# Latent attention: probabilities turned into two f16 parts, three f16 products with the latents, and the loop over head pairs turned by two tiles

## The chip, the cores and the metric

One core of a Trainium2 chip runs the whole kernel in one launch. The metric is the device time of one execution in microseconds (us); the median of several runs is what counts. TensorE multiplies matrices into PSUM, VectorE and ScalarE read PSUM and write SBUF, GpSimd works on SBUF alone, SyncE issues the loads.

## The reference

Two layers, each a gated cross attention followed by a gated feed-forward block, on 4 x 256 tokens of width 256. The change lies in the attention of the second layer, a latent attention with 16 heads over a context of 256 latents of width 64 per batch:

```python
q_big = apply_rope(einsum('bshk,hkq->bshq', (x @ Wq.T), w_kc_q))     # 192 wide per head
kv_r  = apply_rope(kv_c)                                             # latents, 64 wide
q_r   = einsum('bshq,hqr->bhsr', q_big, W_qr)
k_r   = einsum('bld,hdr->bhlr', kv_r, W_kr)
attn  = softmax(einsum('bhsr,bhlr->bhsl', q_r, k_r), axis=-1)
ctx_c = einsum('bhsl,bld->bhsd', attn, kv_r)
ctx   = einsum('bhsd,hkd->bhsk', ctx_c, w_kc_kv)                     # then @ Wo.T
```

## The kernel before

The attention stage treats the heads in 8 pairs `p` (0 to 7) and the 1,024 tokens in 8 tiles `t` of 128 (two tiles for each batch `b`). Every engine has its own program, and within an engine the order is the one written down; a wait for a semaphore holds all that stands behind it on that engine. For one tile of one pair the chain is:

1. TensorE `scores` (L887): four f16 products of 256 columns into bank SC + t % 2.
2. VectorE (L1068): the row minimum `low` of both heads.
3. ScalarE `softmax` (L956): two exponentials with their sums.
4. VectorE (L1073): the reciprocal `inv`.
5. GpSimd `normalise` (L1011): `PB` times `inv`.
6. TensorE `turn` (L896): four transposes of 128 x 128 in f32 into the single bank PTB.
7. ScalarE `turned` (L965): a copy of the bank to `PTS`, f32, which frees the bank (`t_ok`).
8. After two tiles, TensorE `attend` (L904): the latents `KV` (f32, 64 columns) are stationary, `PTS` moves, one product for each half of the tokens and each head; the two heads write the two halves of the partitions of bank CXB.
9. `attended`: ScalarE takes the f16 high part `XCH` (L972), VectorE the rest `XCL` (L1058).

In between, the next pair's queries are made: TensorE `queries` (L863, six f16 products of 512 columns for each tile), VectorE `rotate` (L1030, two multiplications of 96 x 512), GpSimd `rotated` (L1003, two sums), TensorE `to_context` (L876), whose result ScalarE and VectorE split into `Q` (L950, L1049). It runs twice for a pair, for n = 0 (tokens 0 to 511) and n = 1. The weights of the pair after the next are folded in six steps `fold` 0 to 5 (L856) through one PSUM bank, FO. Steps 0, 1 and 5 leave it in two parts: ScalarE takes the high one, VectorE the rest, and VectorE's part releases the next step (`fold_ok`).

The function `pair` gives the order within a pair on each engine. On TensorE, tile t does `scores`, `queries` of the next pair, at t = 1 `to_context` for n = 1, `fold` t (t below 6), at t = 3, 5, 7 `attend` of an earlier batch, and `turn` of tile t - 1. After tile 7 come `to_context` of the next pair for n = 0, `turn` of tile 7 and `attend` of batch 3. On VectorE, tile t does L1068, `rotate`, then L1073, then its shares of `to_context`, `fold` and `attended`. Pair 6 has no folds; pair 7 has neither folds nor queries, and TensorE does products of the output (L130) in their place. In the rows, lines L139 to L160 are the fold products, L182 is VectorE's share of a fold.

## Time and profile before

| | us |
|---|---|
| median of 3 runs | 545.38 (543.02 to 547.01) |
| the profiled execution, time | 546.3 |
| its span, first to last instruction | 544.6 |
| PE busy | 493.6 (91%) |
| DVE busy | 321.5 (59%) |
| ACT busy | 249.2 (46%) |
| POOL busy | 182.0 (33%) |

PE is TensorE, DVE is VectorE, ACT is ScalarE, POOL is GpSimd. The span leaves out 1.7 us around the instructions. The first layer runs up to about 130 us, the attention of the second from there to about 401 us, and its mixture of experts after that. Times in the rows are counted from the start of the span. A matmul's end is modelled and overlaps the next one's start, so that distances between starts tell more than durations.

### The profile page before, as it was taken

To read this page: it belongs to the slowest core of one execution; us is meant where nothing else is said; L and a number is where in the kernel's file an instruction comes from. 1 tells how busy PE (TensorE), PEld (TensorE's weight loads), DVE (VectorE), ACT (ScalarE), POOL (GpSimd) and SP (SyncE) were. 2 spreads that over 40 slices of the span, in tenths; PEclk is the share of its full clock that TensorE was granted. 3 is DMA by queue.
4 is the path that set the end of the run, shared out by engine and by line. 5 is a ranking of instruction groups with operands and counts; after the bars stand their busy time and mean duration, and the time that the engine had idled before them with its cause. 6 is when DMAs were issued, how large, how long until landed. Compare 5 with 4: busy or idle time off the path is not lost. (4 is left out here: it accounts for less than half of the span.)

```text
span 544.6 us, 9443 instructions
## 1 busy us (share of the span) xinstructions
PE 493.6 (91%) x3202; PEld 345.1 (63%) x3202; DVE 321.5 (59%) x881; ACT 249.2 (46%) x598; POOL 182.0 (33%) x181
## 2 busy tenths in 40 slices
PE   4989999986889899998989899898979869999997
PEld 2667878774346555665656566464756536899986
DVE  4998799632567676775767677583456690222202
ACT  4673464452046566665666656565644300322200
POOL 4141220311355566464556646574320000000000
PEclk9996999999799999999999999999999869999999
DMA  8722000000000202020020000000039000088002
GB/s 261 227 66 70 2 1 1 1 2 0 0 1 3 67 1 68 1 67 1 3 64 0 0 0 0 1 1 1 1 110 304 24 1 1 1 255 239 1 1 78
DMA packets 41298, 26.25 MB, mean 48 GB/s; under 512 B 10048, under 2 KB 40816, under 8 KB 41264
## 3 DMA queue, kind: packets, MB, share of 16 engines
q1 hardware_dynamic: 41264, 25.81, 16.3%
q8 instruction: 20, 0.33, 0.2%
q14 instruction: 14, 0.11, 0.1%
HBM read 24.75 MB, written 1.05 MB: 47 GB/s over the span
## 5 line engine op out<-in xcount | busy, mean ns | idle before, releaser
L1014 POOL TENSOR_TENSOR PB<-PB,inv 128x512 f32<-128x512 f32 x64 | 66.5, 1039 | 102.9 <-DVE inv L1073 102.9
L960 ACT ACTIVATE PB<-ps,low 128x256 f32<-128x256 f32 x128 | 59.4, 469 | 54.4 <-DVE low L1068 54.2
L1039 DVE TENSOR_TENSOR TM<-ps,cosq 96x512 f32<-96x512 f32 x64 | 43.8, 684 | 28.1 <-PE ps L870 26.9
L870 PE MATMUL ps<-XH,CH 128*96 128x512 f16 x128 | 49.9, 390 | 2.6 <-POOLq L1001 2.6
L870 PE MATMUL ps<-XL,CH 128*96 128x512 f16 x128 | 49.5, 387 | 0.0
L870 PE MATMUL ps<-XH,CL 128*96 128x512 f16 x128 | 49.5, 387 | 0.0
L1008 POOL TENSOR_TENSOR RO<-TM 96x512 f32<-96x512 f32 x32 | 40.5, 1265 | 21.0 <-DVE TM L1040 21.0
L1068 DVE TENSOR_REDUCE low<-ps 128x2 f32<-128x512 f32 x64 | 43.6, 682 | 3.8 <-PE ps L892 3.4
L909 PE MATMUL ps<-PTS,KV 128*64 128x256 f32 x256 | 34.4, 389 | 11.8 <-ACT PTS L968 11.8
L1040 DVE TENSOR_TENSOR TM<-ps,sinq 96x512 f32<-96x512 f32 x64 | 43.3, 676 | 0.0
L900 PE MATMUL ps<-ident,PB 128*128 128x128 f32 x256 | 40.9, 282 | 0.8 <-ACT PTS L968 0.8
L358 POOL TENSOR_TENSOR HT<-GL,MS 128x512 f32<-128x512 f32 x16 | 20.3, 1278 | 63.8 <-ACT MS L630 48.8
L1054 DVE TENSOR_TENSOR Q<-ps,Q 64x512 f16<-64x512 f32 x32 | 22.0, 689 | 32.6 <-ACT Q L953 32.3
L900 PEld LDWEIGHTS ps<-ident,PB 128*128 128x128 f32 x256 | 28.2, 141 | 20.0 <-issue 14.6
L968 ACT ACTIVATE PTS<-ps 128x512 f32<-128x512 f32 x64 | 38.2, 597 | 5.6 <-PE ps L900 3.9
L1009 POOL TENSOR_TENSOR RO<-TM 96x512 f32<-96x512 f32 x32 | 40.5, 1265 | 0.0
L953 ACT ACTIVATE Q<-ps 64x512 f16<-64x512 f32 x32 | 18.9, 591 | 31.1 <-PE ps L883 30.7
L892 PE MATMUL ps<-KH,Q 128*128 128x256 f16 x128 | 31.5, 273 | 1.6 <-DVE Q L1054 1.6
L539 PE MATMUL ps<-XT,W1T 128*128 128x256 f32 x128 | 32.6, 406 | 0.0
L883 PE MATMUL ps<-RO,M 96*64 96x512 f32 x128 | 31.0, 605 | 1.1 <-POOL RO L1009 1.1
L909 PEld LDWEIGHTS ps<-PTS,KV 128*64 128x64 f32 x256 | 16.2, 136 | 24.5 <-issue 14.5
L892 PE MATMUL ps<-KL,Q 128*128 128x256 f16 x128 | 31.4, 273 | 0.0
(220 smaller groups left out, 994.4 us busy)
## 6 DMA issues: line engine op xcount, KB each, us to landing
EG<-in_L_ffn_W_gate_dram SPq DMA_DIRECT2D x10, 384.0 KB, 4.3
EU<-in_L_ffn_W_up_dram SPq DMA_DIRECT2D x10, 384.0 KB, 5.1
ED<-in_L_ffn_W_down_dram SPq DMA_DIRECT2D x10, 384.0 KB, 5.8
w<-in_L_ffn_W_dram SPq DMA_DIRECT2D x2, 1024.0 KB, 8.3
WQ<-in_L_xattn_Wq_dram SPq DMA_DIRECT2D x8, 256.0 KB, 2.7
WO<-in_L_xattn_Wo_dram SPq DMA_DIRECT2D x8, 256.0 KB, 3.0
WCQ<-in_L_xattn_w_kc_q_dram SPq DMA_DIRECT2D x8, 192.0 KB, 2.7
X<-in_x_dram SPq DMA_DIRECT2D x2, 512.0 KB, 4.0
```

The source lines that it names most:

```text
L870: mm = pe.matmul(g.ps[0:HALF, QA + a, :], cx[:, k, h * DQ + a * HALF:h * DQ + (a + 1) * HALF], xx[:, k, 512 * n:512 * n + 512], start=(k = ...
L892: mm = pe.matmul(g.ps[:, SC + t % 2, S * h:S * h + S], Q[h][u][:, t * P:(t + 1) * P], kx[:, S * (t // 2):S * (t // 2) + S], start=(m == 0) ...
L900: mm = pe.transpose(g.ps[:, PTB, j * P:(j + 1) * P], PB[t % 2][:, j // 2, (j % 2) * P:(j % 2 + 1) * P], g.ident[:, :])
L909: mm = pe.matmul(g.ps[DC * h:DC * h + DC, CXB, 0:S], g.KV[:, 2 * b + j, 0, :], PTS[b % 2][:, 2 * h + j, :], start=(j == 0), stop=(j == 1))
L960: e = act.activation(PB[t % 2][:, h, :], g.ps[:, SC + t % 2, h * S:(h + 1) * S], ACT.Exp, bias=low[:, t % 2, h:h + 1], scale=-1.0, accum_o ...
L968: act.activation(PTS[t // 2 % 2][:, :, (t % 2) * P:(t % 2 + 1) * P], g.ps[:, PTB, :].rearrange("p (j n) -> p j n", j=4), ACT.Copy).then_in ...
L1008: pool.tensor_tensor(RO[:, n, h, 0, :], tm[:, 0, :], tm[:, 2, :], ALU.subtract).then_inc(sum_ok, 1)
L1009: pool.tensor_tensor(RO[:, n, h, 1, :], tm[:, 3, :], tm[:, 1, :], ALU.add).then_inc(sum_ok, 1)
L1014: pool.tensor_tensor(PB[t % 2][:, :, :], PB[t % 2][:, :, :], inv[:, t % 2, :].unsqueeze(2).broadcast_to([P, 2, S]), ALU.mult).then_inc(nor ...
L1039: dve.tensor_tensor(batches(TM[st % 2][:, c, :]), src, over(g.cosq[:, a, :]), ALU.mult)
L1040: dve.tensor_tensor(batches(TM[st % 2][:, s, :]), src, over(g.sinq[:, 1 - a, :]), ALU.mult).then_inc(rope_ok, 1)
L1068: dve.tensor_reduce(low[:, t % 2, :], g.ps[:, SC + t % 2, :].rearrange("p (h s) -> p h s", h=2), AX.X, ALU.min).then_inc(low_ok, 1)
```

## The change

- The turned probabilities leave PSUM as two f16 parts. ScalarE `turned` writes part 0, 256 times the value, in f16; a new VectorE step `turned` writes part 1, the remainder, and only that frees the bank PTB (`t_ok`). ScalarE's copy signals the new semaphore `t_hi`.
- GpSimd makes two f16 parts `KVP` of the latents in the first layer: a copy, and a subtraction ahead of `fold_second`.
- `attend` does three f16 products (high with high, high with low, low with high) where it had one f32 product: 12 instead of 4. `attended` scales back by 1/256 on both engines.
- The loop over pairs is turned by two tiles. A turn of the loop now does tiles 2 to 7 of a pair (`step`) and then tiles 0 and 1 of the next (`cross`). `turn` of tile 7 stands in tile 0 of the next pair, `attend` of batch 3 in tile 1, with the next pair's scores and queries ahead of them.
- `to_context` for n = 0 moves on TensorE and ScalarE from behind tile 7 into tile 5, on VectorE into tile 6.
- Folds 0 to 4 move from tiles 0 to 4 into tiles 3 to 7 on TensorE and ScalarE, fold 5 from tile 5 into tile 0 of the next pair. VectorE's shares of folds 0 and 1 stand in tiles 4 and 5, one tile later than TensorE's.
- On VectorE the order within a tile becomes L1068, the new `turned` of tile t - 2, the reciprocal, and only then `rotate`; then its shares of `to_context`, `fold` and `attended`.

```diff
+UPP = 256.0
...
+                pool.tensor_copy(g.KVP[:, 0, :, :], g.KV[:, :, 0, :]).then_inc(kvp_ok, 1)
...
+                pool.wait_ge(kvp_ok, 1)
+                pool.tensor_tensor(g.KVP[:, 1, :, :], g.KV[:, :, 0, :], g.KVP[:, 0, :, :],
+                                   ALU.subtract).then_inc(kvp_ok, 1)
...
-        PTS = two("PTS", [P, 4, 2 * P])
-        FIRST = 5
+        PTS = two16("PTS", [P, 2, 4, 2 * P])
+        FIRST, AHEAD = 5, 5
...
-        def pairs(eng, body):
-
+        HEAD, TILES = range(0, 2), range(2, NT)
+        LAST = NT - 1
+
+        def pairs(eng, step, cross):
+
+            for t in HEAD:
+                step(0, 0, t, True, False)
             with eng.Fori(0, (PAIRS - 2) // 2, 1) as it:
                 for u in range(2):
-                    body(it * 2 + u, u, True, True)
-            body(PAIRS - 2, 0, False, True)
-            body(PAIRS - 1, 1, False, False)
+                    for t in TILES:
+                        step(it * 2 + u, u, t, True, True)
+                    for t in HEAD:
+                        cross(it * 2 + (u + 1), 1 - u, t, True, True)
+            for t in TILES:
+                step(PAIRS - 2, 0, t, True, False)
+            for t in HEAD:
+                cross(PAIRS - 1, 1, t, False, False)
+            for t in TILES:
+                step(PAIRS - 1, 1, t, False, False)
...
                     for j in range(2):
-                        for h in range(2):
-                            mm = pe.matmul(g.ps[DC * h:DC * h + DC, CXB, 0:S], g.KV[:, 2 * b + j, 0, :],
-                                           PTS[b % 2][:, 2 * h + j, :], start=(j == 0), stop=(j == 1))
+                        for m, (kv, part) in enumerate(((0, 0), (0, 1), (1, 0))):
+                            for h in range(2):
+                                mm = pe.matmul(g.ps[DC * h:DC * h + DC, CXB, 0:S], g.KVP[:, kv, 2 * b + j, :],
+                                               PTS[b % 2][:, part, 2 * h + j, :], start=(j == 0 and m == 0),
+                                               stop=(j == 1 and m == 2))
                     mm.then_inc(cx_ps, 1)
...
-                def pair(p, u, folds, asks):
-                    for t in range(NT):
-                        scores(p, u, t)
-                        if asks:
-                            queries(p + 1, 1 - u, t)
-                        else:
-
-
-                            if t == 0:
-                                pe.wait_ge(cx_ok, 4 * p + CXOK0)
-                            output_share(pe, g, t // 2, range(0, 4) if t % 2 == 0 else range(4, PAIRS - 1))
-                        if t == 1:
-                            to_context(p, u, 1)
-                        if folds and t < 6:
-                            fold(p + 2, u, t)
-                        if t in (3, 5, 7):
-                            attend(p, t // 2 - 1)
-                        if t >= 1:
-                            turn(p, t - 1)
+                def shares(t):
+
+                    output_share(pe, g, t // 2, range(0, 4) if t % 2 == 0 else range(4, PAIRS - 1))
+
+                def step(p, u, t, asks, folds):
+                    scores(p, u, t)
                     if asks:
+                        queries(p + 1, 1 - u, t)
+                    else:
+                        shares(t)
+                    if t == 1:
+                        to_context(p, u, 1)
+                    if t == AHEAD and asks:
                         to_context(p + 1, 1 - u, 0)
-                    turn(p, NT - 1)
-                    attend(p, B - 1)
+                    if folds and t >= 3:
+                        fold(p + 2, u, t - 3)
+                    if t in (3, 5, 7):
+                        attend(p, t // 2 - 1)
+                    if t >= 1:
+                        turn(p, t - 1)
+
+                def cross(p, u, t, asks, folds):
+
+                    scores(p, u, t)
+                    if asks:
+                        queries(p + 1, 1 - u, t)
+                    else:
+                        if t == 0:
+                            pe.wait_ge(rope_ok, 8 * PAIRS + ROPE0)
+                            pe.wait_ge(cx_ok, 4 * p - 2 + CXOK0)
+                        shares(t)
+                    if t == 0:
+                        if folds:
+                            fold(p + 1, 1 - u, FOLDS - 1)
+                        turn(p - 1, LAST)
+                    else:
+                        to_context(p, u, 1)
+                        attend(p - 1, B - 1)
+                        turn(p, 0)
 
                 pe.wait_ge(credit, 1)
                 for t in range(NT):
                     queries(0, 0, t)
                     if t == FIRST:
                         to_context(0, 0, 0)
-                pairs(pe, pair)
+                pairs(pe, step, cross)
+                turn(PAIRS - 1, LAST)
+                attend(PAIRS - 1, B - 1)
...
-                    act.activation(PTS[t // 2 % 2][:, :, (t % 2) * P:(t % 2 + 1) * P],
+                    act.activation(PTS[t // 2 % 2][:, 0, :, (t % 2) * P:(t % 2 + 1) * P],
                                    g.ps[:, PTB, :].rearrange("p (j n) -> p j n", j=4),
-                                   ACT.Copy).then_inc(t_ok, 1)
+                                   ACT.Copy, scale=UPP).then_inc(t_hi, 1)
 
                 def attended(p, b):
                     act.wait_ge(cx_ps, 4 * p + (b + 1 + CXPS0))
                     act.activation(g.XCH[:, bass.ds(p, 1), S * b:S * b + S], g.ps[:, CXB, 0:S],
-                                   ACT.Copy).then_inc(cx_hi, 1)
-
-                def pair(p, u, folds, asks):
-                    for t in range(NT):
-                        softmax(p, t)
-                        if t == 1:
-                            to_context(p, u, 1)
-                        if folds and t < 6:
-                            fold(p + 2, u, t)
-                        if t in (3, 5, 7):
-                            attended(p, t // 2 - 1)
-                        if t >= 1:
-                            turned(p, t - 1)
-                    if asks:
+                                   ACT.Copy, scale=1.0 / UPP).then_inc(cx_hi, 1)
...
+                def step(p, u, t, asks, folds):
+                    softmax(p, t)
+                    if t == 1:
+                        to_context(p, u, 1)
+                    if t == AHEAD and asks:
                         to_context(p + 1, 1 - u, 0)
-                    turned(p, NT - 1)
-                    attended(p, B - 1)
+                    if folds and t >= 3:
+                        fold(p + 2, u, t - 3)
+                    if t in (3, 5, 7):
+                        attended(p, t // 2 - 1)
+                    if t >= 1:
+                        turned(p, t - 1)
+
+                def cross(p, u, t, asks, folds):
+
+                    softmax(p, t)
+                    if t == 0:
+                        if folds:
+                            fold(p + 1, 1 - u, FOLDS - 1)
+                        turned(p - 1, LAST)
+                    else:
+                        to_context(p, u, 1)
+                        attended(p - 1, B - 1)
+                        turned(p, 0)
...
-                    dve.tensor_tensor(g.XCL[:, bass.ds(p, 1), cols], g.ps[:, CXB, 0:S],
-                                      g.XCH[:, bass.ds(p, 1), cols], ALU.subtract).then_inc(cx_ok, 1)
-
-                def pair(p, u, folds, asks):
-                    for t in range(NT):
-                        dve.wait_ge(s_ps, 8 * p + (t + 1))
-                        dve.tensor_reduce(low[:, t % 2, :], g.ps[:, SC + t % 2, :].rearrange("p (h s) -> p h s", h=2),
-                                          AX.X, ALU.min).then_inc(low_ok, 1)
-                        if asks:
-                            rotate(p + 1, t)
-                        dve.wait_ge(exp_ok, 8 * p + (t + 1 + EXP0))
-                        dve.reciprocal(inv[:, t % 2, :], tot[:, t % 2, :]).then_inc(inv_ok, 1)
-                        if t == 1:
-                            to_context(p, u, 1)
-                        if folds and t < 6:
-                            fold(p + 2, u, t)
-                        if t in (3, 5, 7):
-                            attended(p, t // 2 - 1)
+                    dve.scalar_tensor_tensor(out=g.XCL[:, bass.ds(p, 1), cols], in0=g.ps[:, CXB, 0:S],
+                                             scalar=1.0 / UPP, in1=g.XCH[:, bass.ds(p, 1), cols], op0=ALU.mult,
+                                             op1=ALU.subtract).then_inc(cx_ok, 1)
+
+                def lowest(p, t):
+
+                    dve.wait_ge(s_ps, 8 * p + (t + 1))
+                    dve.tensor_reduce(low[:, t % 2, :], g.ps[:, SC + t % 2, :].rearrange("p (h s) -> p h s", h=2),
+                                      AX.X, ALU.min).then_inc(low_ok, 1)
+
+                def inverse(p, t):
+
+                    dve.wait_ge(exp_ok, 8 * p + (t + 1 + EXP0))
+                    dve.reciprocal(inv[:, t % 2, :], tot[:, t % 2, :]).then_inc(inv_ok, 1)
+
+                def turned(p, t):
+
+                    dve.wait_ge(t_hi, 8 * p + (t + 1))
+                    cols = slice((t % 2) * P, (t % 2 + 1) * P)
+                    dve.scalar_tensor_tensor(out=PTS[t // 2 % 2][:, 1, :, cols],
+                                             in0=g.ps[:, PTB, :].rearrange("p (j n) -> p j n", j=4), scalar=UPP,
+                                             in1=PTS[t // 2 % 2][:, 0, :, cols], op0=ALU.mult,
+                                             op1=ALU.subtract).then_inc(t_ok, 1)
+
+                def step(p, u, t, asks, folds):
+                    lowest(p, t)
+                    if t >= 2:
+                        turned(p, t - 2)
+                    inverse(p, t)
                     if asks:
+                        rotate(p + 1, t)
+                    if t == 2:
+                        to_context(p, u, 1)
+                    if t == AHEAD + 1 and asks:
                         to_context(p + 1, 1 - u, 0)
-                    attended(p, B - 1)
+                    if folds and t in (4, 5):
+                        fold(p + 2, u, t - 4)
+                    if t in (4, 6):
+                        attended(p, t // 2 - 2)
+
+                def cross(p, u, t, asks, folds):
+
+                    lowest(p, t)
+                    turned(p - 1, NT - 2 + t)
+                    inverse(p, t)
+                    if asks:
+                        rotate(p + 1, t)
+                    if t == 0:
+                        attended(p - 1, B - 2)
+                        if folds:
+                            fold(p + 1, 1 - u, FOLDS - 1)
+                    else:
+                        attended(p - 1, B - 1)
 
                 dve.wait_ge(credit, 1)
                 dve.wait_ge(g.d_ropeq, 32)
@@ -1087,7 +1170,11 @@
                     rotate(0, t)
                     if t == FIRST + 1:
                         to_context(0, 0, 0)
-                pairs(dve, pair)
+                pairs(dve, step, cross)
+                turned(PAIRS - 1, NT - 2)
+                attended(PAIRS - 1, B - 2)
+                turned(PAIRS - 1, LAST)
+                attended(PAIRS - 1, B - 1)
...
+            g.KVP = mb("KVP", [P, 2, NT, DC], F16)
```

## Rows read from the trace of the kernel before

**Rows 1.** Windows view, attention loop: length, busy us (instructions) per engine, clock, DMA, GB/s

```profile
159.80:393.50 233.70, 220.31 (x1410) 135.69 (x1410) 153.84 (x310) 145.52 (x411) 132.45 (x118) 1.00 0.06 16
```

**Rows 2.** Timeline of TensorE, pair 2: start us, us, instruction, idle before

```profile
223.24 1.94 PE L883 MATMUL ps<-RO,M 96*64 96x512 f32 x8
...
225.11 0.92 PE L139 MATMUL ps<-WCQ,WQ 128*128 128x192 f32 x4
...
226.30 0.27 PE L892 MATMUL ps<-KH,Q 128*128 128x256 f16 x1
...
228.50 0.38 PE L143 MATMUL ps<-ident,WQR 96*128 96x96 f32 x2 [0.30 <-DVE CL L182]
...
229.02 0.66 PE L900 MATMUL ps<-ident,PB 128*128 128x128 f32 x4
...
229.51 0.27 PE L892 MATMUL ps<-KH,Q 128*128 128x256 f16 x1
...
231.77 1.08 PE L909 MATMUL ps<-PTS,KV 128*64 128x256 f32 x8
...
232.79 0.65 PE L900 MATMUL ps<-ident,PB 128*128 128x128 f32 x4
...
240.18 0.27 PE L892 MATMUL ps<-KH,Q 128*128 128x256 f16 x1
...
241.91 0.60 PE L900 MATMUL ps<-ident,PB 128*128 128x128 f32 x4
...
249.71 0.65 PE L909 MATMUL ps<-PTS,KV 128*64 128x256 f32 x4 [1.42 <-ACT PTS L968]
```

**Rows 3.** Timeline of TensorE, pair 3: first score product of tile 2

```profile
258.00 0.27 PE L892 MATMUL ps<-KH,Q 128*128 128x256 f16 x1
```

**Rows 4.** Timeline of VectorE, pair 2, tiles 2, 3 and 6

```profile
228.36 0.68 DVE L1068 TENSOR_REDUCE low<-ps 128x2 f32<-128x512 f32 x1
...
228.96 0.68 DVE L1039 TENSOR_TENSOR TM<-ps,cosq 96x512 f32<-96x512 f32 x1
...
230.15 0.15 DVE L1073 RECIPROCAL inv<-tot 128x2 f32<-128x2 f32 x1
...
230.22 0.67 DVE L1068 TENSOR_REDUCE low<-ps 128x2 f32<-128x512 f32 x1
...
240.82 0.69 DVE L1068 TENSOR_REDUCE low<-ps 128x2 f32<-128x512 f32 x1
```

**Rows 5.** Timeline of VectorE and GpSimd, pair 7, one tile without rotation

```profile
388.94 0.69 DVE L1068 TENSOR_REDUCE low<-ps 128x2 f32<-128x512 f32 x1 [0.24 <-PE ps L892]
...
390.72 0.17 DVE L1073 RECIPROCAL inv<-tot 128x2 f32<-128x2 f32 x1 [1.09 <-ACT PB L960]
...
390.96 1.04 POOL L1014 TENSOR_TENSOR PB<-PB,inv 128x512 f32<-128x512 f32 x1 [1.14 <-DVE inv L1073]
```

**Rows 6.** Groups by line, VectorE, attention loop: busy us, mean ns, idle before

```profile
L1054 DVE TENSOR_TENSOR Q<-ps,Q 64x512 f16<-64x512 f32 x30 | 20.7, 689 | 32.6 <-ACT Q L953 32.3
...
L182 DVE SCALAR_TENSOR_TENSOR CL<-ps,CH 128x384 f16<-128x384 f32 x11 | 6.1, 551 | 0.4
...
L182 DVE SCALAR_TENSOR_TENSOR NL<-ps,NH 128x256 f32 x6 | 2.4, 400 | 0.0
```

**Rows 7.** Timeline: pair 0's tile 2 on TensorE, and the last VectorE row of the stage

```profile
162.88 0.27 PE L892 MATMUL ps<-KH,Q 128*128 128x256 f16 x1
...
400.33 0.42 DVE L1062 TENSOR_TENSOR wide<-ps,wide 128x256 f16<-128x256 f32 x1 [3.33 <-ACT wide L974]
```

**Rows 8.** Timeline of GpSimd in the first layer

```profile
24.84 4.31 POOL L349 TENSOR_SCALAR wide<-X,mix 128x256 f32<-128x256 f32 x8 [11.82 <-DVE mix L732]
...
31.64 0.92 POOL L368 TENSOR_TENSOR CL<-FS,CH 128x384 f16<-128x384 f32 x1 [2.49 <-ACT FS L614]
```

**Rows 9.** Windows view around a fall of TensorE's clock, columns as in rows 1

```profile
36.70:40.10 3.40, 1.18 (x9) 0.73 (x7) 3.36 (x15) 2.39 (x7) 1.57 (x3) 1.00 0.70 193
...
40.00:56.00 16.00, 15.08 (x70) 11.72 (x71) 13.39 (x56) 6.38 (x12) 2.52 (x3) 0.68 0.25 74
```

More of the change, by code:

```diff
@@ L1016, in normalise @@
                                        ALU.mult).then_inc(norm_ok, 1)
-                def pair(p, u, folds, asks):
-                    for t in range(NT):
-                        normalise(p, t)
-                        if asks and t % 2 == 1:
-                            rotated(p + 1, t // 2)
+                def step(p, u, t, asks, folds):
+                    normalise(p, t)
+                    if asks and t % 2 == 1:
+                        rotated(p + 1, t // 2)
+                def cross(p, u, t, asks, folds):
+                    step(p, u, t, asks, folds)
                 for st in range(4):
                     rotated(0, st)
-                pairs(pool, pair)
+                pairs(pool, step, cross)
             @block.vector
@@ L1084, in _, with cross @@
+                def cross(p, u, t, asks, folds):
+                    lowest(p, t)
[9 more added lines that the diff above has]
+                        attended(p - 1, B - 1)
                 dve.wait_ge(credit, 1)
```

15 lines of the change are left out of this document (8 added, 7 removed).

## The prediction

> **What bounds the kernel now.** I read the windows view of the attention loop first. TensorE is busy 220.3 of 233.7 us at full clock, VectorE 153.8 (66%) [rows 1]. Then the timeline of one pair on TensorE: the reader is to see that its blocks follow each other almost without a gap and that the pattern repeats after 258.00 - 226.30 = 31.70 us [rows 2, 3]. Distances between starts give the price of each block. A plain tile (240.18 to 241.91) has scores and queries, S+Q = 1.73, for 4 x 256 + 6 x 512 = 4,096 columns, which makes 0.108 for 256 columns in f16. The others are to_context 1.87 (223.24 to 225.11), fold 1 0.75 (225.11 to 226.30 less one turn of 0.44), fold 2 0.52, turn 0.49 (229.02 to 229.51), attend 1.02 (231.77 to 232.79) [rows 2]. The one large gap is 1.42 us at 249.71, at the end of the pair, where attend of batch 3 waits for ScalarE's copy; there is one of 0.30 at fold 2 [rows 2]. Each gap is about 0.16 longer than shown, because of the modelled end of the matmul before it, so about 2.0 us of a pair are idle. So TensorE bounds the loop, at 29.7 us of work in 31.7.
>
> VectorE is the engine to look at next. Where work is queued, its big steps start 0.60 apart: minimum 0.60, the two multiplications of rotate 1.19, reciprocal 0.07, a tile in 1.86 [rows 4]. The time that matters is the one hidden there: in pair 7, where no rotate stands between them, the reciprocal starts 1.78 after the minimum, of which 1.09 is a wait for ScalarE's exponentials [rows 5]. Before, rotate fills that wait.
>
> **The change part by part.**
>
> TensorE's work. An attend of now runs its two heads side by side: each f32 instruction takes twice 0.108 for 256 columns, eight would need 1.73 in a row, and the block takes 1.02 = 4 x 0.215 + 0.16 [rows 2]. Twelve f16 products side by side make 6 x 0.108 + 0.17 = 0.83; one behind the other they would make 12 x 0.108 + 0.17 = 1.47. No row shows f16 products of 64 columns. I take 0.83, by the attend row, since only the type differs, and keep 1.47 as a bound. This takes 4 x 0.19 = 0.8 us of work from a pair. The turned order also puts scores and queries between turn 7 and attend 3, so that the gap at the end of a pair loses its cause. If TensorE still bounded the loop, a pair would take 29.7 - 0.8 = 28.9.
>
> VectorE's work. The new turned has 512 columns. The same instruction takes 0.400 with 256 and 0.551 with 384 [rows 6], so 0.70, or 0.61 from start to start. ScalarE's copy and its 64 instructions stay as they are.
>
> VectorE's order. What costs is where the reciprocal stands. A tile is now minimum (0.60), turned (0.61), then the rest of the wait for the exponentials: the reciprocal starts 1.80 after the minimum whatever turned costs between nothing and 1.2, then rotate. That is 1.80 + 0.07 + 1.20 = 3.07 a tile against 1.86 [rows 4, 5]. Turned is hidden; rotate no longer is. The extras follow behind rotate: to_context 1.38 [rows 6], fold 0.48, fold 5 and attended 0.37 each. Without any wait for TensorE a pair costs VectorE 8 x 3.07 + 2 x 1.38 + 2 x 0.48 + 0.37 + 4 x 0.37 = 30.1 us, more than TensorE's 28.9 and near the 31.7 of now.
>
> The fold chain. TensorE's fold 1 stands in tile 4 and needs `fold_ok` of fold 0, which VectorE gives behind rotate of tile 4, because its share stands one tile later. With L for the start of VectorE's minimum (0.64 after the start of scores, 240.18 to 240.82 [rows 2, 4]), TensorE has its queries out at L + 1.09 and then holds until L + 3.07 + 0.56 + 0.06 = L + 3.69. Queued behind are fold 1, turn 3 and the scores of tile 5, for which VectorE waits in turn. So the two engines take turns instead of overlapping: the next minimum comes at 3.69 + 0.75 + 0.49 + 0.64 = 5.57. Tile 5 repeats it with fold 2, with to_context hidden in the wait: 3.69 + 0.52 + 0.83 + 0.49 + 0.64 = 6.17. Without these two holds the tiles would take 3.44 and 3.96.
>
> A pair, minimum to minimum, is then: tile 2 4.45 (3.07 and to_context); tile 3 3.31 (attend needs turned of tile 1, at L + 1.35, then 0.83 + 0.49 + 0.64); tile 4 5.57; tile 5 6.17; tile 6 4.80 (3.07, to_context, attended); tile 7 3.31; next tile 0 3.81 (3.07, attended, fold 5); next tile 1 3.99 (VectorE waits for attend 3 behind to_context, then ScalarE's part). The sum is 35.4 us, 3.7 more than now.
>
> The stage. It runs from the minimum of tile 2 in pair 0 (162.88 + 0.64 = 163.5) to 400.75, 237.2 us [rows 7]. Pair 0's first tiles lose their two folds, which brings that start to 162.9. Then six turns of the loop, 6 x 35.4 = 212.5; the rest of pair 6 without folds, 4.45 + 3.31 + 3.44 + 3.96 + 4.80 + 3.31 = 23.3; pair 7, without rotate, at 2.48 a plain tile (1.35 for turned, 0.49, 0.64) and 3.31 one with attend: 2.48 + 4.59 + 3 x 2.48 + 2 x 3.31 = 21.1 up to its last minimum, and then 7.8 for the last chain (minimum, exponentials, norm, turn, ScalarE's copy, turned, attend, both attended). The end is 162.9 + 212.5 + 23.3 + 21.1 + 7.8 = 427.6, 26.8 us later than now.
>
> What costs nothing. The two new GpSimd steps of the first layer lie before waits of 11.8 and 2.5 us, and the dearer one should be near 1.2 (0.92 with 384 columns) [rows 8]; uncovered they would cost 2. Loads of the fourth and later pairs start after fold 5, which comes some 11 us later, and still have nine tiles before fold 0 wants them; that cover is over 25 us. Everything behind the stage is as it was.
>
> **A rule of the skill against the change.** The 1.02 of the attend row leaves no room for loads of the stationary latents between products [rows 2]. The Trainium skill (TensorE: Matmul & The Clock Gate, Part 3) says that a load overlaps running products only where the row groups differ, and here both heads use all rows. By it each of twelve loads of 64 columns at its P/1.2 ns, 53 ns, would stand in the open, and attend would come to an estimated 1.47, by chance the bound above. The f32 row does not bear that out, so I leave it to the second rival.
>
> **The rivals.**
>
> 1. TensorE stays the bound and the turned loop gives back the gaps: 28.9 a pair, six pairs 17 us, some 3 more in the last two: 526. It needs rotate or the reciprocal not to hold up the minimum of the next tile. For it speaks that TensorE is 94% busy; against it that the order on VectorE is fixed and its chain alone takes 30.1. Chance 0.05.
> 2. Attend runs head after head, 1.47 instead of 0.83. It lies on the path in tiles 3, 5, 7 and 1: 4 x 0.64 x 7 = 18 us, 590. Chance 0.10.
> 3. TensorE's clock falls in the new holds of 2.5 us. In 36.7 to 40.1 TensorE was busy 1.18 of 3.40 us, mostly with transposes, and the clock stood at its lower level, 1.2 GHz, for about 10 us after it (0.68 over 16 us) [rows 9]. The 1.42 us gap at 249.71 had no such effect; the clock of the loop is 1.00 [rows 1, 2]. The new hold is longer than both, but has dense products on both sides. Each fall would cost 2 to 5 us; three in six pairs make 6 to 15, so 578 to 587. Chance 0.20.
> 4. The fold chain holds nobody, because VectorE's share comes before TensorE asks for it. Then tiles 4 and 5 cost 3.44 and 3.96, a pair 31.1, and the gain in the loop pays for the last chain: 26 us less than my sum, 546. Against it: fold 0 on VectorE stands behind the very scores that TensorE issues just before fold 1. Chance 0.07.
>
> **How the numbers follow.** The profiled execution was 546.3, so my sum is 546.3 + 26.8 = 573.1. The median stands 0.9 lower, and I forecast 572. Errors of 0.1 us in each tile's chain would make 5 us. Chance of this case, 566 to 579, 0.58. Range 562 to 591: it takes in rivals 2 and 3 and leaves out 1 and 4. Slower by over 1% (about what a measurement of this kernel can tell from no change): 0.58 + 0.10 + 0.20 = 0.88. Within 1%: most of rival 4, 0.06. Faster by over 1%: rival 1 and the rest of 4, 0.06.
>
> **What the changed profile would show.** Pairs repeat after about 35.4 us. TensorE's busy share of the loop falls from 94% to about 82%, with two holds in each pair before fold 1 and fold 2, released by VectorE's L182 step, the first near 2.5 us. VectorE has a wait of about 0.5 for ScalarE before each reciprocal and a rotate behind it. The attend block takes 0.83. The end of a pair has no gap. I am wrong if the reciprocal comes much sooner than 1.8 after the minimum, if the fold holds are short, or if scores of the next tile wait for something other than VectorE. The last chain of pair 7 should be about 2 us longer than now.

## The result and the profile after

The changed kernel takes 590.0 us (median of 4 runs, 589.0 to 594.4), and the kernel before took 546.2 beside it (4 runs, 543.0 to 551.4): a ratio of 1.083, 95% interval 1.076 to 1.090. The ratio leaves out the run of 551.4, in which the kernel before was in a slower state. The profiled execution took 594.4 with a span of 592.7; its mean granted clock was 0.941, that of the other runs 0.949 to 0.952, which fits its 4 us above the median.

The page of the changed kernel, its first two parts cut to the lines used here, and then the row of the clock from the page of the kernel before:

```profile
span 592.7 us, 9779 instructions
...
PE 503.8 (85%) x3330; PEld 357.3 (60%) x3330; DVE 365.8 (62%) x945; ACT 246.8 (42%) x596; POOL 184.4 (31%) x183
...
PEclk9997999996988988988999899998898997999999
```

```profile
PEclk9996999999799999999999999999999869999999
```

TensorE is busy for 10 us more but in a span that is 48 longer. Each digit of the clock's row is a fortieth of the span, 14.8 us in the changed kernel, whose loop lies in the 12th to the 27th. The kernel before has nines throughout its loop (clock 1.00 in [rows 1]); the changed one has seven eights there. The windows view of the six turns of the loop, from the minimum of tile 2 in pair 0 to that of pair 6, and of the stretches before and after one fall of the clock (columns as in rows 1):

```profile
163.80:393.90 230.10, 189.42 (x1221) 118.74 (x1219) 162.43 (x308) 116.57 (x331) 110.10 (x98) 0.93 0.06 16
...
211.00:214.40 3.40, 0.89 (x5) 0.33 (x3) 2.89 (x7) 1.02 (x4) 2.77 (x3) 1.00 0.00 0
215.40:218.80 3.40, 3.40 (x13) 1.59 (x11) 1.46 (x3) 1.91 (x6) 0.42 (x1) 0.55 0.00 0
```

TensorE is busy 82% of the loop (94% before), and with a granted clock of 0.93 one clock in fourteen is missing. VectorE in the same pattern, tiles 4 and 5 of pair 5 (timeline; compare [rows 4, 5]). L1120 is the minimum, L1132 the new turned, L1126 the reciprocal, L1090 and L1091 rotate, L183 the fold share; the cut row is the share of attended, L1113:

```profile
364.51 0.69 DVE L1120 TENSOR_REDUCE low<-ps 128x2 f32<-128x512 f32 x1 [0.31 <-PE ps L910]
365.12 0.68 DVE L1132 SCALAR_TENSOR_TENSOR PTS<-ps,PTS 128x512 f16<-128x512 f32 x1
366.29 0.17 DVE L1126 RECIPROCAL inv<-tot 128x2 f32<-128x2 f32 x1 [0.49 <-ACT PB L998]
366.48 0.69 DVE L1090 TENSOR_TENSOR TM<-ps,cosq 96x512 f32<-96x512 f32 x1
367.08 0.68 DVE L1091 TENSOR_TENSOR TM<-ps,sinq 96x512 f32<-96x512 f32 x1
367.68 0.54 DVE L183 SCALAR_TENSOR_TENSOR CL<-ps,CH 128x384 f16<-128x384 f32 x1
...
370.70 0.69 DVE L1120 TENSOR_REDUCE low<-ps 128x2 f32<-128x512 f32 x1 [2.15 <-PE ps L910]
```

The reciprocal starts 1.78 after the minimum and waits 0.49, rotate follows it, and after its shares of fold and attended VectorE stands for 2.15 us. TensorE over the same time (L910 scores, L888 queries, L140 fold 1, L918 turn, L928 attend; compare [rows 2]):

```profile
362.61 0.84 PE L928 MATMUL ps<-PTS,KVP 128*64 128x256 f16 x12 [1.81 <-DVE PTS L1132]
363.38 0.66 PE L918 MATMUL ps<-ident,PB 128*128 128x128 f32 x4
...
365.39 0.38 PE L888 MATMUL ps<-XH,CL 128*96 128x512 f16 x1
368.28 0.92 PE L140 MATMUL ps<-WCQ,WQ 128*128 128x192 f32 x4 [2.51 <-DVE CL L183]
369.03 0.78 PE L918 MATMUL ps<-ident,PB 128*128 128x128 f32 x4
369.61 0.42 PE L910 MATMUL ps<-KH,Q 128*128 128x256 f16 x1
369.82 0.42 PE L910 MATMUL ps<-KL,Q 128*128 128x256 f16 x1
```

Fold 1 is held for 2.51 us and starts 0.06 after VectorE's share ends: the two engines take turns. From 369.6 on the scores start 0.21 apart where 0.11 is usual: the clock is at its lower level. The attend block takes 0.77, from 362.61 to the start of the turn at 363.38. The longest waits of the loop (waits view, 163.8 to 393.9: who waited for whom, us in total, times, longest):

```profile
DVE low L1120 <- PE ps L910: 33.1, 24, 3.1
...
PE ps L928 <- DVE PTS L1132: 21.6, 12, 1.8
...
PE ps L140 <- DVE CL L183: 14.5, 6, 2.5
```

### The profile page after: what moved, and what is told of

The parts are those of the page before. It is cut to its first block and busy times, and to the rows that moved or that the text cites. A ratio compares the mean times of both kernels' runs of the same rounds, so it can differ in the third digit from the quotient of the medians.

```text
span 592.7 us, 9779 instructions
## 1 busy us (share of the span) xinstructions
PE 503.8 (85%) x3330; PEld 357.3 (60%) x3330; DVE 365.8 (62%) x945; ACT 246.8 (42%) x596; POOL 184.4 (31%) x183
## 5 line engine op out<-in xcount | busy, mean ns | idle before, releaser
L1063 POOL TENSOR_TENSOR PB<-PB,inv 128x512 f32<-128x512 f32 x64 | 66.5, 1039 | 140.4 <-DVE inv L1126 140.4
L1120 DVE TENSOR_REDUCE low<-ps 128x2 f32<-128x512 f32 x64 | 44.0, 687 | 41.2 <-PE ps L910 40.8
L888 PE MATMUL ps<-XH,CH 128*96 128x512 f16 x128 | 53.7, 420 | 2.7 <-POOLq L1050 2.6
L928 PE MATMUL ps<-PTS,KVP 128*64 128x256 f16 x384 | 28.7, 288 | 29.9 <-DVE PTS L1132 29.9
L888 PE MATMUL ps<-XL,CH 128*96 128x512 f16 x128 | 53.2, 415 | 0.0
L1090 DVE TENSOR_TENSOR TM<-ps,cosq 96x512 f32<-96x512 f32 x64 | 43.9, 686 | 14.4 <-PE ps L888 12.8
L888 PE MATMUL ps<-XH,CL 128*96 128x512 f16 x128 | 52.4, 409 | 0.0
L918 PE MATMUL ps<-ident,PB 128*128 128x128 f32 x256 | 43.6, 295 | 7.3 <-DVE PTS L1132 7.2
L1132 DVE SCALAR_TENSOR_TENSOR PTS<-ps,PTS 128x512 f16<-128x512 f32 x64 | 43.7, 682 | 2.9 <-ACT PTS L1006 2.6
L928 PEld LDWEIGHTS ps<-PTS,KVP 128*64 128x64 f16 x384 | 20.2, 114 | 39.9 <-issue 28.7
L1091 DVE TENSOR_TENSOR TM<-ps,sinq 96x512 f32<-96x512 f32 x64 | 43.3, 677 | 0.0
L1006 ACT ACTIVATE PTS<-ps 128x512 f16<-128x512 f32 x64 | 38.1, 596 | 11.9 <-PE ps L918 10.7
L918 PEld LDWEIGHTS ps<-ident,PB 128*128 128x128 f32 x256 | 29.1, 146 | 22.4 <-issue 22.2
L910 PE MATMUL ps<-KH,Q 128*128 128x256 f16 x128 | 34.9, 296 | 1.5 <-DVE Q L1105 1.5
L910 PE MATMUL ps<-KL,Q 128*128 128x256 f16 x128 | 35.1, 296 | 0.0
```

Of the source, the lines that this page charges most:

```text
L888: mm = pe.matmul(g.ps[0:HALF, QA + a, :], cx[:, k, h * DQ + a * HALF:h * DQ + (a + 1) * HALF], xx[:, k, 512 * n:512 * n + 512], start=(k = ...
L910: mm = pe.matmul(g.ps[:, SC + t % 2, S * h:S * h + S], Q[h][u][:, t * P:(t + 1) * P], kx[:, S * (t // 2):S * (t // 2) + S], start=(m == 0) ...
L918: mm = pe.transpose(g.ps[:, PTB, j * P:(j + 1) * P], PB[t % 2][:, j // 2, (j % 2) * P:(j % 2 + 1) * P], g.ident[:, :])
L928: mm = pe.matmul(g.ps[DC * h:DC * h + DC, CXB, 0:S], g.KVP[:, kv, 2 * b + j, :], PTS[b % 2][:, part, 2 * h + j, :], start=(j == 0 and m == 0),
L1063: pool.tensor_tensor(PB[t % 2][:, :, :], PB[t % 2][:, :, :], inv[:, t % 2, :].unsqueeze(2).broadcast_to([P, 2, S]), ALU.mult).then_inc(nor ...
L1090: dve.tensor_tensor(batches(TM[st % 2][:, c, :]), src, over(g.cosq[:, a, :]), ALU.mult)
```

## Experiments

The tiles below are distances between starts of VectorE's minimum, in us, taken from the timeline. Each row is one pair of the loop as it ran, and the row of e1 is the one pair of its loop without a fall of the clock.

```
tile                       2     3     4     5     6     7    next 0  1     pair
forecast                  4.45  3.31  5.57  6.17  4.80  3.31  3.81  3.99   35.4
changed kernel, pair 4    4.73  3.45  6.23  6.57  5.05  3.31  3.85  4.36   37.6
e10 (holds filled), 2     4.73  3.45  5.59  6.09  5.04  3.32  3.85  4.35   36.4
e1 (shares early), 3      4.70  3.52  3.96  4.27  5.05  3.31  3.98  4.41   33.2
e4 (rotate first), 2      4.01  3.45  5.08  5.58  4.54  3.32  3.31  4.89   34.2
e5 (both), 2              4.00  3.45  3.45  4.86  4.53  3.32  3.31  4.89   31.8
e6 (both, f32 parts), 5   3.94  2.63  2.96  4.91  4.54  2.28  3.32  4.89   29.5
```

The row of the changed kernel has one fall of the clock in it, in tile 4. Times of pairs differ by some tenths with the clock and between even and odd pairs.

**e1: VectorE's fold shares one tile earlier.**

```diff
-                    if folds and t in (4, 5):
-                        fold(p + 2, u, t - 4)
+                    if folds and t in (3, 4):
+                        fold(p + 2, u, t - 3)
```

> VectorE takes its share of folds 0 and 1 one tile earlier, in the tile in which TensorE makes them. Theory (TensorE and VectorE take turns at folds 1 and 2): the two holds vanish, tiles 4 and 5 take about 3.6 and 4.1 us from minimum to minimum where they took 6.2 and 6.7, six pairs give some 31 us back with the clock falls that followed the holds: about 558. Rival (the new VectorE step turned, or the late rotate, is what costs): 580 or more. Rival (the clock falls come anyway and are the main loss): 575 to 590, with as many falls as before.

569.5 us, ratio to the kernel before 1.044 (1.040 to 1.048), so 20.5 less than the changed kernel, where 31 were expected. The holds went, and tiles 4 and 5 took 3.96 and 4.27, near the 3.6 and 4.1 expected. What stayed are falls of the clock, now at the wait of attend in tile 7: five from pair 0 to pair 5 and one in pair 6, where the changed kernel had nine and two. A pair with one took 34.5 to 34.9 where the table shows 33.2 for the one without. The theory of the hold stands. The rival about the falls is right in that they come without the hold, but about half of them went, and the time lies below its 575.

**e2 and e10: the holds filled.** Before fold 1 TensorE does ten products of 512 columns into the idle bank QP; e10 also does five before the attend of tile 7. Nobody reads them.

```diff
+                    if folds and t == 4:
+                        for k in range(10):
+                            pe.matmul(g.ps[:, QP, :], g.XH[:, 0, 0:P], g.XH[:, 1, 0:512], start=True, stop=True)
                     if folds and t >= 3:
                         fold(p + 2, u, t - 3)
+                    if folds and t == 7:                                  # e10 alone
+                        pe.wait_ge(qc_ok, 2 * p + 3 + QC0)
+                        for k in range(5):
+                            pe.matmul(g.ps[:, QP, :], g.XH[:, 0, 0:P], g.XH[:, 1, 0:512], start=True, stop=True)
```

> TensorE fills its hold in tile 4 with ten products of 512 columns (2.15 us) that nobody reads, and holds as long as before. Theory (the hold is set by VectorE, and the clock falls on top cost about 1 us each, some nine of them): the falls that come in tiles 4 and 5 go, the hold stays, 580 to 585. Rival (the clock is the main loss): 570 or less. Rival (the clock costs nothing, since TensorE waits anyway): 590.

590.4 us, 1.081 (1.077 to 1.085): no change, outside the theory's 580 to 585, and the number of the last rival, but not for its reason, as e10 shows. Tiles 4 and 5 took 5.60 and 6.09 in every pair, no fall in them any more; now five pairs of the loop have one in tile 7, where the changed kernel had two. The mean clock of the four runs is 0.949 to 0.955, like that of the changed kernel outside the profiled execution. TensorE in pair 4 of e2 (timeline; L949 is the fill):

```profile
324.25 2.32 PE L949 MATMUL ps<-XH 128*128 128x512 f16 x10
326.93 0.92 PE L140 MATMUL ps<-WCQ,WQ 128*128 128x192 f32 x4 [0.35 <-DVE CL L183]
...
341.30 1.22 PE L928 MATMUL ps<-PTS,KVP 128*64 128x256 f16 x12 [1.77 <-DVE PTS L1135]
342.45 1.11 PE L918 MATMUL ps<-ident,PB 128*128 128x128 f32 x4
```

The fill fits into the hold and fold 1 starts no later. In tile 7 the clock falls during the attend that follows the wait of 1.77 us, and attend takes 1.15 instead of 0.77. In pair 3 the same wait, 1.78, has no fall after it. So e10 filled that one too:

> The changed kernel, with TensorE's hold before fold 1 filled with ten products of 512 columns and its wait before the attend of tile 7 with five, read by nobody. Theory (falls of the clock move to the longest idle stretch left, and cost 10 to 15 us in all): no falls in the loop, every pair 36.6 us, 576 to 582. Rival (the clock costs nothing, since TensorE waits anyway): 590. Rival (falls go on elsewhere): 586 to 590 with falls in other tiles.

582.5 us, 1.068 (1.063 to 1.073). Its loop over six turns has no fall (windows view; 230.1 us in the changed kernel):

```profile
162.00:380.80 218.80, 195.39 (x1310) 120.02 (x1309) 161.78 (x307) 116.83 (x331) 109.99 (x98) 1.00 0.06 17
```

The falls of the loop cost 230.1 - 218.8 = 11.3 us in the profiled execution. The median fell by 7.5, to just above the expected 576 to 582; two falls are left in pair 6, which has no fill, and the profiled execution of the changed kernel had a lower clock than its others. TensorE does 2.15 + 1.08 us more in each pair and the kernel is faster.

**e3: the turned loop with the f32 parts of before.** ScalarE's copy gives `t_ok`, VectorE's turned goes, attend is that of before; loop, folds and VectorE's order are those of the change.

```diff
-        PTS = two16("PTS", [P, 2, 4, 2 * P])
+        PTS = two("PTS", [P, 4, 2 * P])
...
-                    if t >= 2:
-                        turned(p, t - 2)
                     inverse(p, t)
```

> The turned loop, folds and order as after the change, but probabilities leave PSUM as one f32 copy and attend does the f32 products of before; VectorE's step turned is gone. Theory (turned is hidden in the wait for the exponentials, attend is 0.2 shorter in f16): holds and falls stay, attends cost 0.2 more each, a few waits of turn and attend go: 583 to 592. Rival (the new VectorE step is the cause of the loss): 560 or less.

578.4 us, 1.059 (1.056 to 1.063): 11.6 less, outside what I expected and far from the rival. The bare VectorE tile is 3.06, so turned itself is hidden there as forecast. But tiles 3, 7 and 1 take 3.06, 3.06 and 3.75 to 4.3 instead of 3.45, 3.31 and 4.36: attend does not wait behind a minimum. That wait was in my sum, but I had not listed it as a cost of the parts. The 11.6 also understates what the parts cost at full clock: in e3 TensorE comes to fold 1 earlier and is held for 4.5 to 4.8 us, and the one fall of each pair then lasts about 7 us where those of the changed kernel last about 3.5. Tile 4 takes 7.15, against 5.59 in e10. TensorE in pair 2 of e3:

```profile
249.18 1.65 PE L140 MATMUL ps<-WCQ,WQ 128*128 128x192 f32 x4 [4.82 <-DVE CL L183]
```

**e4: rotate before the reciprocal.**

```diff
-                    inverse(p, t)
                     if asks:
                         rotate(p + 1, t)
+                    inverse(p, t)
```

> VectorE does rotate before the reciprocal, as in the kernel before, all else as after the change. Theory (rotate is no longer hidden in the wait for the exponentials): tiles bound by VectorE get 0.6 to 0.7 us shorter, some five of eight, and the hold at fold 1 shrinks by as much: 565 to 572. Rival (the place of the reciprocal doesn't matter because TensorE bounds): 588 to 592. Rival (the later reciprocal delays turn): 595 or more.

567.7 us, 1.038 (1.032 to 1.045), 22.3 less, within the theory's range. Against the row of e10, which like that of e4 has no fall in it, the tiles bound by VectorE, 2, 4, 5, 6 and 0, lost 0.50 to 0.72 each, and tile 1 gained 0.54. Not all of the 22.3 is VectorE's order. The six turns took 209.0 us in the profiled execution, 21.1 less than in the changed kernel. By the table some 13 of them are the tiles, 6 x (36.4 - 34.2); the other 8 or so are falls, of which the loop has two instead of nine.

**e5: both orders mended. e6: both, with the f32 parts.**

> Both edits: VectorE's share of folds 0 and 1 in TensorE's tile, and rotate before the reciprocal. Theory (these two orders on VectorE hold the loop, the turned loop itself is sound): tiles of 4.0, 3.45, 3.4, 4, 4.5, 3.3, 3.3 and 4.9, 30.8 a pair, 545 to 550. Rival (the two savings are the same wait seen twice): 560 to 567. Rival (falls of the clock stay in every pair, at the waits of attend for turned): 552 to 558.

> As the run with both edits, but with f32 parts and the attend of before; VectorE's turned is gone. Theory (turned is on the path where attend and turn wait for it, 1.4 us a pair): 6 to 12 less than the run with both edits, 537 to 543, below the kernel before. Rival (once TensorE bounds, f16 attends win 0.8 us a pair): 3 to 6 more than the run with both edits.

e5 took 551.6 us, 1.011 (1.008 to 1.014), just above the expected 545 to 550: 38.4 less than the changed kernel, against 20.5 + 22.3 for the edits alone, so they are two costs and not one. It has one fall in the loop, so some 10 of the 38 are falls that went. That fall comes behind a wait of attend in tile 7 of pair 1 which each pair of e5 has (TensorE, timeline):

```profile
214.83 0.85 PE L928 MATMUL ps<-PTS,KVP 128*64 128x256 f16 x12 [1.26 <-DVE PTS L1132]
```

Tile 5, with to_context, folds and attend on TensorE, took 4.86 and not the 4 that I expected. e6 took 527.3 us, 0.965 (0.963 to 0.968): 24 less than e5, where the theory had 6 to 12, and the fastest kernel of this study. The windows of e5 and e6 over two pairs (226 to 290):

```profile
226.00:290.00 64.00, 57.77 (x409) 37.46 (x407) 51.98 (x102) 38.77 (x112) 36.64 (x33) 1.00 0.11 29
```

```profile
226.00:290.00 64.00, 64.00 (x408) 40.51 (x406) 47.85 (x98) 41.26 (x123) 39.72 (x36) 1.00 0.10 29
```

In e6 TensorE is busy without a gap; in e5, with less to do, it is busy 90%. So the f16 parts make the loop leave TensorE's bound. Of their 24 us some 16 are the six turns of the loop (31.8 against 29.5 a pair, and the one fall), some 5 lie in pairs 6 and 7 (first to last minimum 53.1 against 48.4), and 3 behind the last minimum.

**e7: the f16 parts in the loop of before.** The kernel before, with `KVP`, both `turned` and the three f16 products; VectorE does turned of tile t - 2 behind the minimum, and at the end of a pair as follows.

```diff
+                    turned(p, NT - 2)
                     if asks:
                         to_context(p + 1, 1 - u, 0)
+                    turned(p, NT - 1)
                     attended(p, B - 1)
```

> The kernel before with its own loop and fold order, but with the two f16 parts, VectorE's turned after the minimum two tiles later, and three f16 products in attend. Theory (the parts alone cost little; what costs is VectorE's order and the fold shares): attends give 0.8 a pair back, turned lengthens the chain at the end of a pair by 0.7 to 1.4: 545 to 553. Rival (the parts are a main cause): 560 or more.

577.5 us, 1.059 (1.054 to 1.065), 31 more than before: the theory's 545 to 553 is wrong, the rival right. The end of the pair is where it starts. TensorE and VectorE of e7 at the end of pair 2 (timeline; L906 turn, L916 attend, L1078 turned, L1062 to_context):

```profile
251.96 0.66 PE L906 MATMUL ps<-ident,PB 128*128 128x128 f32 x4
255.56 1.49 PE L916 MATMUL ps<-PTS,KVP 128*64 128x256 f16 x12 [2.95 <-DVE PTS L1078]
```

```profile
253.32 1.39 DVE L1062 TENSOR_TENSOR Q<-ps,Q 64x512 f16<-64x512 f32 x2 [1.80 <-ACT Q L961]
254.74 0.69 DVE L1078 SCALAR_TENSOR_TENSOR PTS<-ps,PTS 128x512 f16<-128x512 f32 x1
```

Turned of tile 7 stands behind both halves of to_context, and the 1.42 us gap of before [rows 2] is 2.95. A pair without a fall takes 33.8 to 34.0, over 2 more than before; with the falls that follow the gap, up to 36.7. In the profiled execution the six turns are 20.8 us longer than before (210.0 against 189.1), some 12 of them by the chain and some 8 by four falls.

**e8 and e9: turned ahead of the minimum**, in e5 and in the changed kernel.

```diff
-                    lowest(p, t)
                     if t >= 2:
                         turned(p, t - 2)
+                    lowest(p, t)
```

> As the run with both edits and f16 parts, and VectorE does turned of tile t - 2 ahead of the minimum of tile t. Theory (attend and turn wait for turned only because it stands behind a minimum that waits for scores; 1.0 us in tile 7, 0.8 in tile 3, 0.5 in tile 4): most of the 2.3 us a pair between the two runs comes back and the f16 attends keep their 0.8: 524 to 532. Rival (the 0.61 us that turned takes on VectorE are the cost, wherever it stands): 548 to 552.

> The changed kernel with that edit alone. Theory (with the reciprocal ahead of rotate, turned was hidden in the wait for the exponentials and now adds 0.6 to each tile bound by VectorE, while tiles 3, 7 and 1 lose their wait): the two about cancel, 586 to 600. Rival (the place of turned alone is the loss): 570 or less.

e8 took 558.7 us, 1.021 (1.013 to 1.029), and its loop ran like that of e5: 31.6 a pair, last minimum at 398.3 where e5 has 399.2. The theory that the place behind the minimum is what costs has fallen, and in the loop the rival, that VectorE's 0.6 us cost wherever they stand, fits: tile 3 still takes 3.5 and tile 7 3.4, now because turned waits for ScalarE's copy with the minimum behind it, and VectorE's 0.6 us stand in front of the minimum. That e8 is 7 slower than e5, and above the rival's range too, lies after the attention, in code that is the same, where e8 met a lower clock; why it did is open. The windows of e5 and then e8, from 408 us to the end:

```profile
408.00:548.80 140.80, 130.91 (x1023) 106.19 (x1021) 55.17 (x166) 27.88 (x53) 1.41 (x5) 0.96 0.34 98
```

```profile
408.00:556.70 148.70, 138.85 (x1017) 113.38 (x1015) 54.44 (x164) 27.21 (x52) 0.20 (x1) 0.91 0.32 93
```

e9 took 627.2 us, 1.149 (1.145 to 1.154), worse than I expected. Tiles 2 and 6 got their 0.6, as forecast; tiles 4 and 5 went to between 6.9 and 7.7, because turned of tile 3 waits, with the minimum behind it, for a copy that comes after the hold of the fold (a wait of 2.89 us in pair 5). Many of these tiles met the lower clock as well: 14 falls of the clock lie in pairs 0 to 5.

**e11, e12 and e13: turned's time and turned's waits, each alone**, on the base of e6 (527.3). e11 adds a step of 512 columns on SBUF data behind each minimum, for which nobody waits. e12 puts VectorE between ScalarE's copy and `t_ok` with a step on two columns. e13 adds the step of 512 columns out of PSUM, inside rotate.

```diff
+                def turned(p, t):                                         # e12
+                    dve.wait_ge(t_hi, 8 * p + (t + 1))
+                    dve.tensor_tensor(SP[:, :], g.KV[:, 0, 0, 0:2], g.KV[:, 0, 1, 0:2],
+                                      ALU.subtract).then_inc(t_ok, 1)
...
+                    dve.scalar_tensor_tensor(out=batches(SP[:, :]), in0=src, scalar=UPP, in1=over(g.cosq[:, a, :]),
+                                             op0=ALU.mult, op1=ALU.subtract).then_inc(t_hi, 1)     # e13
```

> The run with both edits and f32 parts (527), plus one VectorE step of 512 columns behind each minimum, on data that lies in SBUF already, for which nobody waits. It tells the time that turned takes on VectorE from the waits for it. Theory (the waits are the cost): 527 to 533, since VectorE has room. Rival (the time is the cost): 545 to 552, as the run with both edits and f16 parts.

> The same base (527), but VectorE stands between ScalarE's copy and the release of the bank: at the place of turned it waits for the copy and does a step on two columns that gives t_ok. The waits of turn and attend for VectorE, without its 0.6 us. Theory (the waits behind a minimum are the cost): 540 to 548, as tiles 3, 4 and 7 get their wait less 0.6. Rival (the time is the cost): 527 to 532.

> The base with both edits and f32 parts (527), plus one VectorE step of 512 columns for each tile with queries, out of PSUM into f16 as turned has it, placed inside rotate, for which nobody else waits. In the run with the extra step on SBUF data that step took 0.89 us in the mean and GpSimd's steps grew from 1.04 to 1.20, so it was dearer than turned. Theory (turned's 0.6 us and the waits for it are two bounds of about the same height, each alone near 31.4 a pair): 538 to 548. Rival (the time alone costs nothing, only the port it shared with GpSimd did): 527 to 532.

e11: 556.4 us, 1.021 (1.013 to 1.029). e12: 545.2, 0.998 (0.995 to 1.002). e13: 544.9, 1.000 (0.997 to 1.002). The theory of e11 fell, those of e12 and e13 came in. The pairs take 31.5, 31.4 and 31.1 against 29.5 in e6 and 31.8 in e5. So either half alone, the time or the waits, brings 1.6 to 2.0 of the 2.3 us of a pair, and in e12 and e13 18 of the 24 us. I read this as two bounds of about the same height that VectorE's order sets above TensorE's: taking one away leaves the other, and gives back 6 or 7 us.

e11's 556.4 is too high for turned's time. Most of its 11 us above e12 lie behind the last minimum, where e11 met a lower clock, as e8 did. The windows of e11 and then e12 from there to the end:

```profile
395.41:553.50 158.09, 145.49 (x1057) 117.21 (x1055) 59.77 (x176) 31.66 (x62) 4.20 (x12) 0.89 0.31 87
```

```profile
394.30:543.70 149.40, 136.57 (x1057) 109.34 (x1055) 57.55 (x176) 31.52 (x62) 3.83 (x12) 0.95 0.32 92
```

Its step was also dearer than turned. The groups by line of e11, VectorE and GpSimd (L1062 is the multiplication that took 1.04 us before [rows 5], 1,039 ns in the mean of the changed kernel), and one such step with the GpSimd sum that was running when it started:

```profile
L1129 DVE SCALAR_TENSOR_TENSOR SP<-KV,KVP 128x512 f16<-128x512 f32 x64 | 56.9, 889 | 0.2
```

```profile
L1062 POOL TENSOR_TENSOR PB<-PB,inv 128x512 f32<-128x512 f32 x63 | 75.7, 1203 | 89.6 <-DVE inv L1124 89.6
```

```profile
256.24 1.27 POOL L1057 TENSOR_TENSOR RO<-TM 96x512 f32<-96x512 f32 x1
...
256.68 1.38 DVE L1129 SCALAR_TENSOR_TENSOR SP<-KV,KVP 128x512 f16<-128x512 f32 x1
```

In e13 the step took 677 ns and GpSimd kept its 1,039.

```profile
L1091 DVE SCALAR_TENSOR_TENSOR SP<-ps,cosq 96x512 f16<-96x512 f32 x56 | 37.9, 677 | 0.0
```

## Why the prediction came out as it did

**The sign, VectorE's order and the fold chain were right, the size was too small:** 26.6 us forecast, 44 measured, 590 at the top edge of the range. The account for the profiled execution, with each term from the starts of the minima:

```
forecast                                                           573.1
attention starts later (tile 2 of pair 0 at 163.8, forecast 162.9)  +0.9
chain of a pair 36.5 without falls (e10: 218.8 / 6), forecast 35.4   +6.3
falls of the clock in six turns, 230.1 - 218.8                     +11.3
pairs 6 and 7 and the last chain, 56.9, forecast 52.2               +4.7
after the attention, 141.9, before 143.8                            -1.9
sum                                                                594.4
```

Of the 4.7, 3.1 are in pair 6, which has two falls, and 1.4 in pair 7. The sum gave tile 1 of pair 7 4.59 without a working; it took 4.85.

**The step that failed is the clock, which the sum left at full throughout.** The term for its falls was put at nothing, on the ground that the hold has dense products on both sides, and three falls at 6 to 15 us were left to the third rival, with 0.20. In the profiled execution there were nine falls from pair 0 to pair 5 and two in pair 6. The nine cost 11.3 us, about 1.3 each, the largest term of the account, and e10, which fills the holds, has none in its loop and a median 7.5 lower. The rival's price holds the 11.3 by luck: three times as many falls as it counted, each below its 2 to 5 us. The dense products did not save the clock: in the stretch ahead of the fall at 215.4 TensorE was busy 0.89 of 3.4 us. Also, I looked at the hold before fold 1 alone, 14.5 us of the loop; attend waits longer in all, 21.6 us, up to 1.8 each time, and in e1 and e2 the falls stand behind that wait in tile 7. The length of one wait does not settle it. After 1.78 us there was none in pair 3 of e2, and after the gap of 1.42 none in the kernel before; in e5, where attend waits 1.26 in tile 7 of every pair of the loop, the clock fell once behind it, in pair 1. What decides between them no run here tells. The Trainium skill (TensorE: Matmul & The Clock Gate, HAM oscillation) describes matmuls that restart at half rate after every wait in a loop; this loop does so at least once in each pair from 0 to 5, after shorter waits than the 3 to 5 us of that example.

**VectorE's order.** The reciprocal does start 1.78 after the minimum and rotate behind it; a bare tile is 3.06, forecast 3.07. e4 confirms the direction, and in the loop a cost of some 13 us without the falls. Tiles 2 and 6 were short by 0.25: in them rotate follows the reciprocal by 0.18 to 0.22 rather than 0.07, to_context follows rotate by 0.71 rather than 0.60, and it takes 1.42. In the odd tiles, behind the same wait, rotate mostly follows by 0.08; the difference is not explained. Tile 1 was short by up to 0.37, the ScalarE part of attended behind a late attend. These small errors are most of the 6.3 us of the chain; the forecast had allowed 5 for them.

**The fold chain.** Forecast 5.57 and 6.17, in e10 5.59 and 6.09; the hold near 2.5 us was 2.51. e1 takes it away. This was the surest part of the sum.

**Turned hidden.** True of its duration, false as a price. Without turned the changed kernel is 11.6 faster, the mended one 24.4. In the sum it stood as the start of attend at L + 1.35; I never asked what the tile would cost without it.

**Attend.** 0.77 (362.61 to 363.38), forecast 0.83. The second rival is out. With it falls, for this case, the rule of the Trainium skill (TensorE: Matmul & The Clock Gate, Part 3) by which twelve loads would stand in the open and make an estimated 1.47: twelve loads and twelve products fit into 0.77.

**The first rival, TensorE's bound at 526,** is not what the change did. e6, where nothing on VectorE or in the folds stands in the way, takes 527.3, which is near 526 partly by luck: e6 has the f32 attends, and its pair of 29.5 is the 29.7 us of work that the prediction counted before, not the rival's 28.9. No run reaches 28.9. The fourth rival, folds that hold nobody, is e1, and needed an edit. The two GpSimd steps cost nothing that shows, as forecast.

**Where the 44 us come from,** by the runs: the two orders on VectorE 38 (590.0 to 551.6), the f16 parts 24 (551.6 to 527.3), and the turned loop itself gives 19 back (527.3 against 546.2 before). The division hangs on the order: with the parts taken out first they are 12 (590.0 to 578.4) and the two orders 51 (578.4 to 527.3). Falls of the clock are in all of these numbers but the 19. The parts cost 31 in the loop of before. What stays open is how the cost of the parts divides between time and waits: e12 and e13 fit two bounds of nearly one height, and no run separates them further. Open too is the lower clock behind the attention in e8 and e11, some 9 us.

## What to carry to other kernels

When a loop has one engine near its bound, write down for each step of the next engine what hides it; an operation moved out of a wait costs in each turn what it filled there, here 0.5 to 0.7 us in five of eight tiles and, with the falls of the clock that came with it, 22 us for one changed order. A share of a step that frees a single bank belongs in the same turn as the step itself; one turn later makes two engines alternate. A new evacuation step has two prices, its time and its place in the release of the buffer, and taking one away shows little while the other stands. When forecasting stalls on TensorE, price the clock with them: a fill that nobody reads paid for itself. And when an edit takes stalls away, count the falls before and after, or the clock's share is booked to the edit.

## What the runs showed of the hardware

- TensorE's clock fell behind waits of 1.8 to 2.5 us in the loop of the changed kernel, not behind each of them, and once behind one of 1.26 (e5). Scores then start 0.21 instead of 0.11 apart, and a fall cost about 1.3 us. Filling the holds kept the clock of the loop at 1.00 and gave 7.5 us.
- After holds of 4.5 to 4.8 us (e3) the clock stayed at its lower level for about 7 us, twice as long as in the changed kernel.
- VectorE and GpSimd slow each other when VectorE reads two operands from SBUF: 889 ns for a step that takes 677 out of PSUM (e11, e13), and 1,203 for GpSimd's 1,039. The Trainium skill (SBUF — State Buffer, SBUF: two separate sides) says that such a VectorE operation and a GpSimd one that reads SBUF share a port pair and the later one waits for the whole of the other. The step of 1.38 us at 256.68 agrees: it started while GpSimd's sum ran to 257.51 and ended 0.55 after it.
- Two heads in two column halves of the array run side by side in f16 as in f32: twelve products of 256 columns in 0.77 us.
